# Block sums of the eight-head pass made one chunk later on TensorE

## The reference

```python
h_src = (x @ W_src).reshape(N, H, D); h_dst = (x @ W_dst).reshape(N, H, D)
h_src_e = h_src[src]
e = leaky_relu(h_src_e + h_dst[dst], 0.2)
s = einsum('ehd,hd->eh', e, attn)
m = segment_max(s, dst); exp_ = exp(s - m[dst]); denom = segment_sum(exp_, dst)
msg = h_src_e * (exp_ / (denom[dst] + 1e-8))[..., None]
out = segment_sum(msg, dst) @ W_out + b_out     # then + x, and a norm
```

## Time and profile before

| | |
|---|---|
| median of 3 runs | 15205.29 us (15198.96 to 15227.11) |
| span of the profiled execution | 12943.7 us |
| median less that span | 2261.6 us |
| PE busy, share of the span | 10725.3 us, 83% |
| POOL busy | 9352.2 us, 72% |
| DVE busy | 7913.5 us, 61% |
| ACT busy | 5610.6 us, 43% |

### The profile page before, as it was taken

How to read it: one execution, slowest core, us unless ns; L and a number is a source line. 1 busy time by engine, 2 the same in 40 slices (tenths; PEclk the granted TensorE clock), 3 DMA queues, 4 the chain that set the end, 5 groups by cost and what they waited for, 6 DMA issues and landing times.

```text
span 12943.7 us, 281524 instructions
## 1 busy us (share of the span) xinstructions
PE 10725.3 (83%) x62317; PEld 8649.8 (67%) x62317; DVE 7913.5 (61%) x29130; ACT 5610.6 (43%) x14105; POOL 9352.2 (72%) x8593
## 2 busy tenths in 40 slices
PE   5788887788888878888888886999999878888886
PEld 4666666666666666666666665777777656666664
DVE  7666666666666655555555555333333568888887
ACT  1555555455555553333333335344444543333334
POOL 3777777577777758888888885777777447777775
PEclk7999999899999966666666667555555688889887
DMA  3222222422222224444444445222222222222222
GB/s 96 56 55 55 55 55 55 132 65 56 56 56 56 55 42 39 39 39 39 39 39 39 38 39 131 57 56 56 56 56 56 58 65 62 62 61 63 61 61 61
DMA packets 809108, 749.26 MB, mean 58 GB/s; under 512 B 264686, under 2 KB 691175, under 8 KB 808255
## 3 DMA queue, kind: packets, MB, share of 16 engines
q0 software_dynamic: 453440, 550.05, 24.5%
q1 hardware_dynamic: 354814, 191.38, 5.7%
HBM read 548.62 MB, written 192.13 MB: 57 GB/s over the span
## 4 chain that ended last, share of the span: by engine, by line
PE 52%; issue 9%; DVE 8%; DMA 6%; POOL 2%; ACT 2%; DVEq 2%; SPq 0%; POOLq 0%; ACTq 0%
PE bank L721 13%; PE bank L705 7%; PE bank L708 6%; DMA scatter_s<-dst_side 6%; PE bank L706 5%; PE bank L1181 4%; PE bank L1187 3%; PE bank L730 3%; PE bank L690 2%; PE bank L1196 2%; POOL scatter_s L1148 2%; DVE agg L929 1%; DVE dst_side L1274 1%; DVE lrelu L884 1%; PE bank L1190 1%
## 5 line engine op out<-in xcount | busy, mean ns | idle before, releaser
L1148 POOL DMA_INDIRECT scatter_s<-dst_side x1664 | 2566.9, 1543 | 555.4 <-DMA scatter_s<-dst_side 240.1
L808 ACT ACTIVATE oh_e<-bank,weight,minus_w 128x128 f32<-128x128 f32 x4992 | 1876.2, 456 | 1465.3 <-PE bank L730 1385.3
L920 DVE SCALAR_TENSOR_TENSOR agg<-agg,rescale,bank 128x130 f32 x4992 | 1680.8, 337 | 1211.0 <-PE bank L721 958.6
L706 PE MATMUL bank<-rows,ident 128*128 128x128 f32 x9984 | 2108.6, 296 | 0.0
L672 POOL DMA_INDIRECT rows<-gather_c,edge_sb x1664 | 1631.9, 981 | 599.6 <-issue 382.3
L672 POOL DMA_INDIRECT rows<-gather_b,edge_sb x1664 | 1605.9, 965 | 608.5 <-issue 314.8
L672 POOL DMA_INDIRECT rows<-gather_a,edge_sb x1664 | 1622.8, 975 | 555.4 <-issue 315.5
L672 POOL DMA_INDIRECT rows<-gather_s,edge_sb x1664 | 1570.3, 944 | 571.3 <-issue 378.7
L721 PE MATMUL bank<-rows,oh_e 128*128 128x130 f32 x9984 | 1873.4, 343 | 54.1 <-DVE agg L920 37.1
L721 PEld LDWEIGHTS bank<-rows,oh_e 128*128 128x128 f32 x9984 | 1601.6, 242 | 268.5 <-issue 230.4
L706 PEld LDWEIGHTS bank<-rows,ident 128*128 128x128 f32 x9984 | 1695.0, 213 | 0.0
(11 more groups left out here) (345 smaller groups left out, 19310.3 us busy)
## 6 DMA issues: line engine op xcount, KB each, us to landing
rows<-gather_a,edge_sb POOLq DMA_INDIRECT x1664
rows<-gather_b,edge_sb POOLq DMA_INDIRECT x1664
scatter_s<-dst_side POOLq DMA_INDIRECT x1664, 3.4
rows<-gather_s,edge_sb POOLq DMA_INDIRECT x1664
rows<-gather_c,edge_sb POOLq DMA_INDIRECT x1664
rows<-scatter_s SPq DMA_DIRECT2D x56, 455.0 KB, 6.1
scatter_s<-zeros SPq DMA_DIRECT2D x64, 390.0 KB, 5.7
edge_sb<-edge_tab SPq DMA_DIRECT2D x520, 40.0 KB
```

The lines of the kernel that those rows point to most:

```text
L706: e.matmul(o, ident[:, :], rows[:, it.slot(), g, 0:P], start=False, stop=True).then_inc(L.side.sem, 1)
L808: e.activation(oh_e[:, g % 8, :], bank[7][:, (g % CH) * P:(g % CH + 1) * P], ACT.Relu, bias=weight[:, it.slot(2, 2), g:g + 1], scale=minus ...
L920: e.scalar_tensor_tensor(old, old, rescale[:, it.slot(2, 2), g:g + 1], sum_bank(g)[:, (g % 2) * AW:(g % 2) * AW + L.aw], ALU.mult, ALU.add ...
L1148: e.indirect_dma_start(scatter_s[k], bass.IndirectOffsetOnAxis(ap=S_.target[:, it.slot(1), g:g + 1], axis=0), S_.summed[:, g % 8, :], None ...
```

## The change

In the eight-head pass PE no longer makes a chunk's block sums in that chunk. It makes chunk c-1's in chunk c, behind chunk c's target sides and distances; chunk 0 makes none; chunk 3 makes those of chunks 2 and 3, one after the other. The other passes stay as they are, and so do all other engines' programs. No instruction is added or removed.

```diff
-                    if two:
+                    if two and not L.wide:
                         for g in range(c * CH, (c + 1) * CH):
                             block_sums(it, g)
+                    if two and L.wide and c:
+                        for g in range((c - 1) * CH, c * CH):
+                            block_sums(it, g)
+                        if c == NCH - 1:
+                            for g in range(c * CH, G):
+                                block_sums(it, g)
```

## The result

The changed kernel took 15580.8 us (median of 5 runs, 15573.24 to 15593.95) against 15217.34 us of the kernel before (5 runs): a ratio of 1.0241, 95% interval 1.0228 to 1.0253. It is 363 us slower. The range (15,540 to 16,200 us) held the time and the direction was right, but the loss was forecast at 645 us (15,850 less 15,205 us).

A forecast was written before the change was run, and what follows sets the result against it. The prediction took a cycle of handovers between PE and DVE to bound the eight-head pass. It added 382 us of waits and 265 us of slow clock to 15205.3 us, giving 15,850 us, range 15,540 to 16,200 us.

The forecast's parts named there:

- What bounds the pass: Eight-head pass: neither PE nor DVE is full; each turn they hand work to each other around one cycle, 20.3 us.
- Nothing is reordered: On PE, matmuls run strictly in program order, so ready block sums cannot overtake a held transpose.
- Chunks 1 and 2: DVE's adds of steps 4 and 8 wait for late block sums: +1.5 us and +2.8 us a turn.
- Chunk 0: DVE's 0.75 us wait moves to its first add: 0.0 us a turn, 1.5 us gained at the loop jump.
- The clock: Two half-clock stretches a turn on PE instead of one, on paths DVE waits for: 2.6 us a turn, 265 us.
- Rival 1: Eight-head pass: new waits alone, the clock costing no more than today: 15,590 us; chance 0.22.
- The sum: Whole kernel: span 12943.7 us plus 382 and 265, with 2261.6 us around it staying: 15,850 us.

The follow-up runs named there:

- the fully filled kernel: Changed kernel plus unused 128-row fp32 products on PE ahead of its three waits: 13432.55 us against 12980.05 us for the kernel before, ratio 1.0347, quick condition.

## Why the prediction was right, and where it was not

**What bounds the pass.** Right. PE and DVE hand work around one cycle, and what was moved lay on it.

**Nothing is reordered.** Right: PE sat 5.0 us in the turn shown at L767, L771 and L774, and no matmul behind them began before they did. At L767 the one-hot matrix of the next side sums had been made by ACT (L800) at 13510.03, 1.9 us before PE went on.

**Chunks 1 and 2.** Right in place and sign, by two ways: moved alone they cost +445 and +282 us in the long condition, and with the scans ahead of the adds the loss goes. The size of the waits at full clock (4.9 us a turn, 382 us in all with the loop jumps) is near what the fully filled kernel has, 5.5 us and +453 us. About half of its turns are 24.6 to 24.9 us, where 20.3 + 4.1 = 24.4 was drawn.

**Chunk 0.** "Sum: 0.0 us" is a term that was too low. In the fully filled kernel DVE waits 1.0 us there on the mean, and 0.8 in about half of the turns, near the 0.7 drawn; in the changed kernel the path is at half clock in many turns, and then it is 2.4 us (26 of 65 turns are over 2 us). Moved alone it made +61 us in the quick condition, where I expected -40.

**The clock.** The step was right, its size not. I counted two stretches of 3.3 us a turn with 1.4 us each, 265 us in all. The longer turn shown has three, about 12 us together, and its last path is slow almost throughout. At a mean clock of 0.81, time at half clock is 2 x 0.19 x 29.4 = 11 us a turn (an estimate; before, at 0.90 and 21.3 us, it is 4). Taking most of it away gave back 350 us. Rival 1, the waits without the clock, has the right number (15,590 us) for the wrong reason: the granted clock did fall, from 0.90 to 0.81.

**The sum.** The step that failed is its base: "what lies around it in the median of the runs is 2261.6 us, and it stays". 3 us lie around it. The two numbers came from two conditions of the chip, and the cost of an edit isn't the same in both: +803 us in the one whose trace I had, where I forecast 647, and +363 and +383 us in the one that was timed. That the time fell into my range is luck: my loss was 156 us too low for the condition I had worked it out for, and it was added to a time of the other, where it was 282 us too high. 15,581 us lies below the 15,700 to 16,050 us that I gave the forecast itself. The turns of 24 to 27 us and the pass of 2870 us that I named came out as neither: 29.4 us a turn in the quick condition, 31.4 in the long one. Nothing in the material of before showed the second condition but that gap of 2262 us, where the execution that has both numbers has 3 us; I should have made it a rival.

Why the change costs less in the long condition isn't shown, as there is no trace of before in it. What bears on it is the kernel with chunk 0 moved alone, which is within 0.5% of before in either and has a trace in both. In the quick one its eight-head turn is 21.9 us, in the long one 27.2 (1471 gathers in 2500 us):

```profile
12300.00:14800.00 2500.00, 1831.66 (x11408) 1500.62 (x11409) 1644.21 (x4663) 720.59 (x1766) 1455.12 (x1471) 0.82 0.18 48
```

The long condition adds 5.3 us to that turn, but only 2.0 us to the changed kernel's (29.4 and 31.4). So the added waits and that condition's delays seem to lie on top of each other in part. How they do was argued, not tried.

## What to carry to other kernels

When two engines pass work round a cycle, moving an instruction behind a wait of its own engine is free only if nothing that this wait needs stands, on the other engine, behind a user of the moved result; follow each moved semaphore once round the whole turn. Order both engines together: here the same move costs 6% with one order on VectorE and 0.1%, not told from nothing, with another, though that other order has a price of 0.7% of its own. A gap that is created ahead of matmuls on the critical path can cost more than its length, since they may then run at 1.2 GHz, as here; filling it with useless products of full size gave back 350 of 803 us.

And compare the span of the profiled execution with the timed median before building on it: here a difference of 2262 us in 15,205 meant that they weren't of the same condition.

## What the hardware showed that was not expected

- Two conditions, 15 to 18% apart for one and the same program (12,936 to 13,013 us and 15,019 to 15,227 us). Four chips were used after the result, each once, one in the long condition and three in the quick one; whether the condition belongs to a chip or to a time isn't shown. In the long one engines start late behind signals that by the issue times should be there, as DVE's add 5.6 us after the products above, and PE stops inside side sums, between steps that share all their waits, here in the first pass of the kernel with chunk 0 moved alone:

```profile
1511.12 0.27 PE L705 MATMUL bank<-dst_side,hT 128*128 x1 [0.67 <-issue]
1511.85 0.27 PE L705 MATMUL bank<-dst_side,hT 128*128 x1 [0.45 <-issue]
1512.57 0.36 PE L706 MATMUL bank<-rows,ident 128*128 128x128 f32 x1 [0.45 <-issue]
1513.99 0.37 PE L706 MATMUL bank<-rows,ident 128*128 128x128 f32 x1 [1.06 <-issue]
```

  What causes it stays open.
- Fillers of 5 rows kept PE nearly as busy as fillers of 128 rows (1592.6 and 1631.6 us of 1900), but the granted clock was 0.84 with the first and 0.97 with the second. The first are bf16 and the second fp32, and their numbers differ too (64 and 22 a turn), so which of these counts is open.
